# Top-2 expert stages: statistics three batches ahead, choice of experts two, gates turned inside the first product

## The reference

```python
t = t + _L1_ffn_ref(_ln_t(t), router_w, router_b, expert_w, expert_b)
# in _L1_ffn_ref
router_probs = softmax(x @ router_w + router_b)          # 8 experts
top_p, top_i = top_k(router_probs, 2)
top_p = top_p / sum(top_p)
expert_out = einsum('bnd,edc->bnec', x, expert_w) + expert_b
gathered = take_along_axis(expert_out, top_i[..., None], axis=2)
return einsum('bnk,bnkc->bnc', top_p, gathered)
```

## Time and profile before

| | us |
|---|---|
| median of 3 runs | 7205.77 (7200.67 to 7206.1) |
| the profiled execution | 7190.95 |
| its span | 7189.3 |
| stage t1 (tokens from DRAM), from its first to its last instruction | about 2288.7 to 3027.5 |
| stage t3 (tokens in SBUF), from its first instruction to the end | about 6324.9 to 7189.3 |

### The profile page before, as it was taken

One profiled execution on the slowest core, in us unless ns is written; L12 is line 12 of the kernel. 1 busy time (PEld: TensorE's weight loads), 2 busy tenths in 40 slices (PEclk: granted clock), 3 DMA queues, 4 the chain that ended last, 5 costly groups with the idle time before them and its releaser, 6 DMA issues. The chain is left out here.

```text
span 7189.3 us, 135354 instructions
## 1 busy us (share of the span) xinstructions
PE 5627.3 (78%) x46688; PEld 3709.5 (52%) x46688; DVE 4337.2 (60%) x8970; ACT 3717.2 (52%) x6916; POOL 1457.5 (20%) x1334
## 2 busy tenths in 40 slices
PE   6776777655697787759997998760899999957787
PEld 4554555225354333349997997250455555523333
DVE  6665666554522778782223344628777777758786
ACT  4554555433543666462224322515677667646664
POOL 3333333423321000060000001403121111121111
PEclk9888888875798888859998999955999999978888
DMA  0110010221232777630000032303666666537666
GB/s 26 31 31 25 25 30 25 71 54 53 81 86 83 239 247 246 208 99 0 0 0 0 0 105 94 89 7 107 92 78 83 86 83 86 73 117 212 210 210 202
DMA packets 793846, 645.72 MB, mean 90 GB/s; under 512 B 496193, under 2 KB 643841, under 8 KB 793421
## 3 DMA queue, kind: packets, MB, share of 16 engines
q1 hardware_dynamic: 792397, 639.01, 36.2%
q0 software_dynamic: 1024, 1.05, 0.1%
HBM read 549.73 MB, written 90.20 MB: 89 GB/s over the span
## 5 line engine op out<-in xcount | busy, mean ns | idle before, releaser
L2306 PE MATMUL sw_pC<-sw_row,sw_wc 128*128 128x128 f32 x10160 | 1159.1, 274 | 56.9 <-DVE sw_row L2181 54.9
L2306 PEld LDWEIGHTS sw_pC<-sw_row,sw_wc 128*128 128x128 f32 x10160 | 1148.6, 191 | 58.2 <-DVE sw_row L2181 55.5
L2740 PE MATMUL sp_pC<-sp_work,sp_bands 64*64 64x512 f32 (+11 forms) x14592 | 985.5, 428 | 43.3 <-issue 43.3
L2740 PEld LDWEIGHTS sp_pC<-sp_work,sp_bands 64*64 64x64 f32 x14592 | 600.3, 133 | 431.9 <-issue 363.9
L2169 DVE SCALAR_TENSOR_TENSOR sw_row<-sw_pC,sw_y 128x128 f32<-128x128 f32 x1016 | 337.1, 332 | 793.3 <-PE sw_pC L2306 793.3
L2679 ACT ACTIVATE sp_pC<-sp_pC,sp_par 128x512 f32<-128x512 f32 x832 | 597.8, 740 | 371.1 <-PE sp_pC L2740 347.6
L1718 DVE TENSOR_TENSOR t_z<-t_z,t_ht 128x1024 f32<-128x1024 f32 x512 | 644.2, 1298 | 144.0 <-DMA t_z<-gate_rows 138.7
L2238 ACT ACTIVATE sw_y<-sw_row 128x128 f32 (+1 forms) x762 | 265.3, 348 | 593.5 <-DVE sw_row L2169 593.5
L1880 PE MATMUL t_pO<-t_z,t_ew 128*64 128x512 f32 x2048 | 553.8, 690 | 4.1 <-DVE t_z L1718 4.1
L2636 DVE TENSOR_TENSOR sp_work<-sp_work,sp_pC 128x512 f32<-128x512 f32 x512 | 351.2, 687 | 168.8 <-ACT sp_pC L2679 168.3
L1850 PE MATMUL t_pT<-t_ident,t_h 128*128 128x128 f32 x1024 | 194.3, 352 | 235.2 <-ACT t_gs L1777 132.1
(11 more groups left out here) (346 smaller groups left out, 11049.4 us busy)
## 6 DMA issues: line engine op xcount, KB each, us to landing
t_z<-gate_rows SPq DMA_DIRECT2D x512, 512.0 KB, 6.0
sp_bands<-windows SPq DMA_DIRECT2D x128, 512.0 KB
c_xs<-tokens SPq DMA_DIRECT2D x128, 256.0 KB, 2.6
cb_xs<-tokens SPq DMA_DIRECT2D x128, 256.0 KB, 2.8
wa_xs<-in_x SPq DMA_DIRECT2D x64, 256.0 KB, 2.8
tokens<-wa_xt SPq DMA_DIRECT2D x128, 128.0 KB, 2.3
tokens<-cb_h SPq DMA_DIRECT2D x64, 256.0 KB, 2.4
t_xs<-tokens SPq DMA_DIRECT2D x32, 512.0 KB, 9.2
```

Source lines behind the costliest of these rows:

```text
L2306: ins = pe.matmul(pC[c][:, 0:2 * P2], wc[:, sweep, m, :], row[1 - par][c][:, :, m:m + P2], start=(m == 0), stop=(m == 4))
L2740: ins = pe.matmul(out[halves[to], :, low * lo:low * hi], band[halves[k], (NV * g + j) % BANDS, q, AT[k][tap], :], v[halves[k], :, low * at ...
```

## The change

On DVE stats and norm move from batch n+2 to n+3 and route from n+1 to n+2; the beat begins with one product, then the gate, then the other seven products with stats between the halves, then norm and route. On ACT root goes ahead of save_mixed(n,1), and gap behind both finishes. On PE turn_gates goes from the head of the beat between q1 and q2 of mix(n,0), and turn(n+2,0) behind mix(n,0). On SP two more load_columns are issued before the first beat in t3, and later ones are two further on. The statements before the first beat follow. No operation is added or taken away.

```diff
--- before.py
+++ after.py
@@ -1610,18 +1610,20 @@
             keep_gates(0)
             for i in range(2):
                 spread_gates(0, i)
+                if rows is not None:
+                    load_columns(7 + i)
             for n in range(NB):
                 if rows is None and XR <= n + 4 < NB:
                     load(n + 4)
-                if rows is not None and 2 * n + 7 < 2 * NB:
-                    load_columns(2 * n + 7)
+                if rows is not None and 2 * n + 9 < 2 * NB:
+                    load_columns(2 * n + 9)
                 if n > 0:
                     store(n - 1)
                 if n + 1 < NB:
                     keep_gates(n + 1)
                     spread_gates(n + 1, 0)
-                if rows is not None and 2 * n + 8 < 2 * NB:
-                    load_columns(2 * n + 8)
+                if rows is not None and 2 * n + 10 < 2 * NB:
+                    load_columns(2 * n + 10)
                 if n + 1 < NB:
                     spread_gates(n + 1, 1)
             store(NB - 1)
@@ -1718,28 +1720,27 @@
                     dve.tensor_tensor(z[:, i, q, :], z[:, i, q, :], ht[:, m.k % HR, i, :], ALU.mult).then_inc(z_ready, 1)
 
             def beat(n):
-                stats_due, route_due = n.plus(2).within(NB), n.plus(1).within(NB)
-                if stats_due:
-                    stats(n.plus(2))
                 weigh(n, 0, [0])
-                if route_due:
-                    route(n.plus(1))
-                weigh(n, 0, [1])
-                if stats_due:
-                    norm(n.plus(2))
-                weigh(n, 0, [2])
-                if route_due:
+                if n.plus(1).within(NB):
                     gate(n.plus(1))
-                weigh(n, 0, [3])
+                weigh(n, 0, [1, 2, 3])
+                if n.plus(3).within(NB):
+                    stats(n.plus(3))
                 weigh(n, 1, range(4))
+                if n.plus(3).within(NB):
+                    norm(n.plus(3))
+                if n.plus(2).within(NB):
+                    route(n.plus(2))
 
             first = Beat(0, 0, 0)
-            stats(first)
-            norm(first)
-            stats(first.plus(1))
+            for i in range(2):
+                stats(first.plus(i))
+                norm(first.plus(i))
+            stats(first.plus(2))
             route(first)
-            norm(first.plus(1))
+            norm(first.plus(2))
             gate(first)
+            route(first.plus(1))
             over_beats(dve, beat, link, 3 + 11 + 1 + 3)
 
         @block.scalar
@@ -1808,13 +1809,13 @@
                     save_turned(m, 1)
                     for i in range(2):
                         save_logits(m, i)
-                save_mixed(n, 1)
                 if n.plus(3).within(NB):
                     root(n.plus(3))
-                finish(n, 0)
+                save_mixed(n, 1)
+                for i in range(2):
+                    finish(n, i)
                 if due:
                     gap(m)
-                finish(n, 1)
 
             def prepare(m, gates_of=None):
                 for i in range(2):
@@ -1829,9 +1830,9 @@
             root(first)
             prepare(first)
             root(first.plus(1))
+            root(first.plus(2))
             gap(first)
             prepare(first.plus(1), first)
-            root(first.plus(2))
             gap(first.plus(1))
             over_beats(act, beat)
 
@@ -1872,9 +1873,11 @@
                 pe.transpose(pT[0][:, 0:128], gates[:, m.k % 2, :, :].rearrange("p e j -> p (e j)"),
                              ident[:, :]).then_inc(gates_turned, 1)
 
-            def mix(m, i):
+            def mix(m, i, gates_of=None):
                 since(pe, oc_saved, 2 * m.n + i - 1)
                 for q in range(4):
+                    if gates_of and q == 2:
+                        turn_gates(gates_of, 4 * m.n + 7)
                     pe.wait_ge(z_ready, 8 * m.n + 4 * i + q + 1)
                     for s in range(2):
                         ins = pe.matmul(pO[i][64 * s:64 * s + 64, :], ew[:, q, :], z[:, i, q, 512 * s:512 * s + 512],
@@ -1906,13 +1909,10 @@
             def beat(n):
                 m = n.plus(2)
                 due = m.within(NB)
-                if n.plus(1).within(NB):
-                    turn_gates(n.plus(1), 4 * n.n + 7)
+                mix(n, 0, n.plus(1) if n.plus(1).within(NB) else None)
                 if due:
-                    turn(m, 0)
-                mix(n, 0)
-                if due:
-                    turn(m, 1)
+                    for i in range(2):
+                        turn(m, i)
                     route(m)
                 mix(n, 1)
                 for i in range(2):
```

## The result

The changed kernel is slower: 7252.14 us (median of 4 runs, 7245.43 to 7256.29) against 7205.94 for the kernel before (4 runs, 7200.67 to 7209.04). The ratio is 1.0064, interval 1.0047 to 1.0081: +46 us, where -8 was forecast.

What follows compares the result with a forecast made beforehand. It took a hand-over loop of ACT and PE, without DVE, to bound the beat. +13 (t1) +5 (t3) -21 (images) -5 (ACT's waits) = -8 us against 7205.8 gave 7198, range 7150 to 7250.

Steps and rivals of the forecast that it cites:

- the three images and ACT's two waits: t3: image stores' delay of DVE nearly all hidden, -21 us; two ACT issue waits at beat heads go, -5 us.
- The walk through t1: Steady t1 beat from exponential to exponential: 20.95 us at the high clock, 22.05 with the low clock; +13 us over 29 beats.
- The clock's term: t1: TensorE's clock falls in the idle time before q1, adding 1.1 us a beat, bounds 0 and 1.7.
- The table load behind finish 1: ACT, each beat: exponential and its table load stand bare behind finish 1, 1.30 us together.
- that rival: ACT: the bare table load costs twice its 1.28 us because ACT drains first; total 7271, chance 0.02.
- Stats, norm and route cost nothing: DVE, steady beat: these and the next q0 end some 2 us before the next exponential, so no cost.
- Its own sign of being wrong: Changed trace: DVE's wait is for something else, t1's clock is over 0.95, or image beats stay above 30 us.
- so I add 0.2: Steady t3 beat: low clock adds 0.2 us, bounds 0 and 1.35, to 23.8 with the join on the chain, giving 24.0.
- The "slower" one: t1 and t3: clock falls before q1 in nearly every beat, low until the transposes; +30 and +37, total 7247, chance 0.18.
- The clock stays high: TensorE in both stages: q0 parts the idle time, t1 beats 20.95 us; total 7160, chance 0.18.
- chain too long: Both stages: chain overestimated, DVE's work nearly bounds, beats 20.0 in t1 and 22.5 in t3; total 7097, chance 0.08.
- The images' rival: t3: a load_columns waiting for its join keeps SP busy, so the images' stall stays; total 7224, chance 0.12.

Runs made afterwards that it cites:

- unused transposes: Changed kernel with twelve transposes of the identity, read by nobody, between q0 and q1 on PE: ratio 1.0025, t1 671.7 us.
- ACT's order alone: Kernel before with only ACT's part of the change (root ahead of save_mixed(n,1), exponential behind both finishes): ratio 1.0140.
- Both cuts of the body: DVE's loop body cut to end with four products in the changed kernel, ratio 1.0058; cut to end with route in the kernel before, ratio 1.0037.
- PE's order undone: Changed kernel with PE's order as before the change, the rest as changed: ratio 1.0148.
- ACT's order undone: Changed kernel with all of ACT's beat as before the change, root included: ratio 1.0158.
- small join: Changed kernel with POOL's addition in t3 cut to one of eight columns, waits, signals and transfers kept: ratio 1.0015, t3 744.8 us.
- that one placement: Changed kernel with only the exponential and its table load back between the two finishes: ratio 0.9868, against 1.0064 with them behind both.

## Why the prediction was wrong

The sum was -8 and the two stages gave +50. Step by step, in us:

| step | forecast | measured |
|---|---|---|
| t1, beats without heads | +13 | (22.20 - 21.60) x 30 = +18 |
| t1, DVE's issue waits at three heads | no term | 82.0 - 3 x 22.20 = +15.4 |
| t3, beats without heads, against 23.83 | +5 | (25.11 - 23.83) x 30 = +38 |
| t3, DVE's issue waits at three heads | no term | 82.3 - 3 x 25.11 = +7.0 |
| t3, the three images and ACT's two waits | -21 and -5 | 30 x 23.83 - 739.9 = -25 |
| starts, first beats and ends of both | 0 | 2.9 - 6.2 + 0.3 + 5.2 - 6.5 + 0.9 = -3.4 |

The rows for t3 add up to the measured +20.3, and all to +50. The -25 is all that stood above 23.83 a beat before the change; what is left of it afterwards is in the 25.11.

**The walk through t1 was right, step by step.** From the exponential, at the high clock and with 0.95 for a low q1, it said: q1 at 2.75, copy of the gates at 4.1 + 0.95 = 5.05, normalise(1) at 5.2, save_mixed at 16.2, finish 1 at 20.0, next exponential at 21.9. The beat shown above has 2.70, 5.01, 5.19, 16.02, 19.79 and 21.70. The unused transposes showed the other half of it, 20.8 at the high clock against 20.95. The clock's term was taken as 1.1 with an upper bound of 1.7; the beats of 22.9 passed that bound, and the mean is 22.20 - 20.95 = 1.25.

**The table load behind finish 1** was right as to its place and cost: 1.28 bare, 1.19 on the path in the kernel with ACT's order alone. It doesn't cost twice its time; that rival is out.

**The first failed step is one that isn't there.** "Stats, norm and route cost nothing: DVE ends them and the next q0 some 2 us before the next exponential." True for a steady beat. At the loop's head the same 2 us stand against 5 to 8 us of issue wait. The earlier trace rows showed such a wait on ACT, and the prediction counted it only as something that goes. It read two of them, where the trace has three. It didn't ask whether DVE would get one from a body that now ends with small operations. Its own sign of being wrong, a wait of DVE for something else than the exponential, came true here. Both cuts of the body showed that this is the cause in t1: 15.0 gone in the one, 26.3 added in the other. +22 of the miss, of which the 15.4 of t1 are shown and the 7.0 of t3 are only counted at the heads.

**The second is a term of the wrong size: t3.** "Here the wait for z hides most of a short low stretch, so I add 0.2." The walk with the join at the high clock was 23.8; measured is 25.11, which leaves 1.3 where the 0.2 stands, nearly its own upper bound of 1.35. Without the join, with the low clock in its rows, the beat is 24.03, with the join 25.11: the wait for z doesn't hide the low stretch, the most of both is paid. The join's own price was right: 1.45 in the walk, 1.41 on the gate product. Only its place was not: 3.2 us behind the exponential in the walk, mostly 0.2 to 3 after the change. It meets the gate in 14 beats, so q1 itself is 1.4 late there and PE idle for 5.6 instead of 4.2 us ahead of it. +33 of the miss.

**Right:** the images (DVE's wait 11.96 to 2.31, though under 2 was said), PE's idle 3.7 ahead of q1 in t1, DVE's wait for the exponential (2.6 in the mean of t1, where 2 was said), the first beats giving back what the starts lose (the exponential of the earlier trace rows waited 6.31 for DVE, now 4.56). ACT's wait for the gates' transpose is there, with 1.5 to 1.9 in t1 where about 1 was said, and up to 3.6 in steady beats of t3.

**The rivals.** The "slower" one gave 7247, near the measured time. Its t3 is right: 25.15 a beat, the join on the chain and the clock's full 1.35, against 25.11. Its t1 is not: a low clock up to the transposes in nearly every beat, +30, where this happens in about every second and the beats without heads gave +18. The heads (+22) were in no rival. That its sum comes near is luck: the 12 us too much in t1 stand against the 22 that it lacks. "The clock stays high" is refuted by 0.87 over t1, and "chain too long" by the walk. The images' rival has a last +5 in its sum for which no source is given; it didn't come.

**What stays open.** What the unused transposes would bring in t3 if they filled the idle stretch there. Why kernels with different orders settle at beats of 23.8 to 23.9: PE's order undone, ACT's order alone, ACT's order undone, t3 with the small join, and t3 of the kernel before. In the first three the beat is about 1 us longer than the walk says (22.8 was expected of the first and 22.6 of the third). That the low clock takes it is argued from 0.85 to 0.86 over most of t1 (0.87 in the changed kernel), and not shown. And why in t3 the cut of the loop body only moves the waits.

## What to carry over

Move a short operation with a dear preparation (here a table load) into a wait of its engine, not behind the last hand-over of the beat: that one placement decided between +0.6% and -1.3%. More than half of this came in the stage with the join, whose start moved against the exponential with it: when one operation moves, look again at what the others now meet. Look at what a hardware loop's body ends with on every engine; long operations that need nothing new belong there, and small chained ones don't. When a walk goes over a stretch with idle TensorE and one with a slowed VectorE, don't let one hide the other unless a row shows it: here the sum was 0.04 off, the choice of 0.2 was 1.1 off.

## What the runs showed of the hardware

- VectorE's wait for issue at a loop's head was 2.9 to 8.8 us behind a chain of small operations, sometimes with a second one behind it (5.92 and 3.42), and at most 0.4 in the kernel before. In each over 2.4 us an 8 KB packet of the kind "instruction" is under way. ScalarE's was 2.45 at most in the kernel before and 5.07 at most in the others.
- Twelve transposes of 1.53 us in all that nobody reads made t1 28.8 us shorter: in the rows shown, 3.72 us of idle time is followed by 0.50 of the clock, 2.26 and 1.99 by q1 in 1.08. In t3, where 4.12 stayed idle behind them, they brought nothing.
- A multiplication of 128 x 128 fp32 values on VectorE took 0.38 us alone and 1.79 beside an addition of 1.62 on GpSimd: it ended 0.23 behind the addition. For t3 this contention was 34 us.
- The table load stands 0.01 to 0.02 us behind the activation before it, 1.28 long, wherever it was put, and 0.01 ahead of the exponential unless that waits for VectorE. The granted clock in t3 rose from 0.84 to 0.89 while its beats became longer, so the mean clock alone is no measure of a stage.
